# Relative values of an attention block formed in turned layout: two 72-row matmuls of 384 columns instead of six over token tiles

## What is computed

```python
attn_probs = jax.nn.softmax(attn_weights, axis=-1)
attn_output = jnp.einsum('bts,bsd->btd', attn_probs, v)
rel_v = _get_relative_embeddings(emb_rel_v, src_len)
rel_weights = _abs_to_rel(attn_probs)
attn_output = attn_output + jnp.einsum('btm,md->btd', rel_weights, rel_v[0])
out = attn_output.reshape(bsz, H, tgt_len, D).transpose(0, 2, 1, 3).reshape(bsz, tgt_len, E)
return out @ Wo + bo
```

## Time and profile before

| | |
|---|---|
| median of 3 runs | 1387.92 us (1380.27 to 1393.97) |
| profiled execution | 1391.63 us, of which the span 1389.6 us |
| mean granted TensorE clock in it | 0.907 |
| busy: PE / PEld / DVE / ACT / POOL | 83 / 58 / 54 / 27 / 17% |
| chain that ended last | PE 31%, issue 28%, DVE 15%, DMA 12%, SPq 5%, ACT 5% |

### The profile page before, as it was taken

The page is one execution under the profiler, slowest core; times in us unless marked ns, Lnnn a source line. Parts: engine busy times, 40 slices in busy tenths (PEclk is TensorE's granted clock), DMA queues, the critical chain, the costliest instruction groups (busy, mean ns, idle before and its releaser), DMA issues.

```text
span 1389.6 us, 16995 instructions
## 1 busy us (share of the span) xinstructions
PE 1160.2 (83%) x5732; PEld 811.2 (58%) x5732; DVE 751.2 (54%) x1579; ACT 370.3 (27%) x599; POOL 234.4 (17%) x258
## 2 busy tenths in 40 slices
PE   5447699878898898988899788987889888997798
PEld 4212378426784377735785267843777357852588
DVE  6337264763548545573556635475455735466333
ACT  1214212062222522043220622115120432206111
POOL 5404120040200302022200402004020212004000
PEclk9667789988899989999899989999899998999889
DMA  6691207302092102901055020921029010650200
GB/s 210 159 199 62 43 5 128 86 1 59 0 161 52 35 23 57 155 1 35 23 96 116 5 54 0 162 51 35 23 51 160 1 35 23 100 112 1 46 0 12
DMA packets 126985, 89.59 MB, mean 64 GB/s; under 512 B 67991, under 2 KB 116504, under 8 KB 126522
## 3 DMA queue, kind: packets, MB, share of 16 engines
q1 hardware_dynamic: 126552, 88.05, 31.4%
q0 software_dynamic: 384, 1.05, 0.3%
HBM read 60.36 MB, written 28.71 MB: 64 GB/s over the span
## 4 chain that ended last, share of the span: by engine, by line
PE 31%; issue 28%; DVE 15%; DMA 12%; SPq 5%; ACT 5%; POOL 2%; POOLq 0%; DVEq 0%; ACTq 0%
DMA scratch<-d_band_t 9%; PE S L881 7%; PE S L754 4%; PE S L902 4%; DVE S L1189 4%; PE S L746 4%; SPq L538 4%; PE S L809 4%; ACT scratch L999 3%; DVE maxima L1168 3%; PE S L710 3%; PE S L794 2%; DMA txt_row<-in_L_txt_W_E,txt_idx 1%; PE S L627 1%; DMA w_d<-in_L_ffn_Wu 1%
## 5 line engine op out<-in xcount | busy, mean ns | idle before, releaser
L1168 DVE TENSOR_REDUCE maxima<-S 128x2 f32<-128x768 f32 x192 | 176.0, 953 | 82.1 <-PE S L754 80.6
L1432 POOL TENSOR_TENSOR bands<-scratch,one 64x432 f32<-64x432 f32 x128 | 119.5, 934 | 585.8 <-ACT scratch L999 580.7
L902 PE MATMUL S<-w_d,hT 128*128 128x256 f32 x768 | 198.6, 412 | 8.1 <-DVE hT L1306 8.1
L902 PEld LDWEIGHTS S<-w_d,hT 128*128 128x128 f32 x768 | 158.6, 210 | 34.1 <-issue 10.8
L746 PE MATMUL S<-k_st,q_st 128*128 128x384 bf16 x384 | 137.1, 357 | 49.1 <-DMA scratch<-d_band_t 34.7
L1189 DVE TENSOR_TENSOR S<-S,bands 64x144 f32<-64x144 f32 x384 | 154.3, 402 | 43.9 <-PE S L794 34.2
L999 ACT ACTIVATE scratch<-S 128x768 f32<-128x768 f32 x192 | 155.6, 811 | 56.5 <-DVE S L1189 49.1
L1037 ACT ACTIVATE silu<-S 128x384 f32<-128x384 f32 x128 | 62.9, 491 | 396.4 <-PE S L881 309.9
L754 PE MATMUL S<-scratch,ident_b 128*128 128x132 bf16 (+1 forms) x384 | 154.5, 402 | 0.0
L1306 DVE TENSOR_TENSOR hT<-silu,S 128x384 f32<-128x384 f32 x128 | 70.6, 552 | 117.9 <-PE S L881 115.7
L794 PE MATMUL S<-q_st,k_st 128*128 128x384 bf16 x384 | 93.2, 342 | 36.4 <-ACT scratch L999 34.8
(11 more groups left out here) (159 smaller groups left out, 1578.4 us busy)
## 6 DMA issues: line engine op xcount, KB each, us to landing
bands<-d_band_s SPq DMA_DIRECT2D x16, 864.0 KB, 8.8
scratch<-d_band_t SPq DMA_DIRECT2D x8, 1632.0 KB, 16.9
d_parts<-scratch SPq DMA_DIRECT2D x48, 192.0 KB, 2.0
q_st<-d_parts SPq DMA_DIRECT2D x48, 192.0 KB
k_st<-d_parts SPq DMA_DIRECT2D x48, 192.0 KB
d_band_w<-bands SPq DMA_DIRECT2D x32, 240.0 KB, 3.8
out<-scratch SPq DMA_DIRECT2D x8, 384.0 KB, 2.7
x_in<-in_x SPq DMA_DIRECT2D x8, 256.0 KB, 3.7
```

The costliest lines, as they stand in the source:

```text
L902: mm = pe.matmul(D[:, i // 2, (i % 2) * E:(i % 2 + 1) * E], hT[:, (FT * e + m) % 3, i * P:(i + 1) * P], w_d[:, e, m, :], start=(m == 0), s ...
L1168: dve.tensor_reduce(dst, S[:, c0:c0 + 2, PAD:PAD + T], AX, ALU.max).then_inc(max_done.sem, 1)
L1432: nc.gpsimd.tensor_tensor(bands[rows, :, :, 2 * pair:2 * pair + 2].rearrange("p i w h -> p h i w"), win, one[rows].unsqueeze(2).unsqueeze( ...
```

## The change

The relative weights are now scaled into two halves of 8 heads (`rel_p`, 72 = 9 x 8 columns each) with two multiplies, each half is turned with three 72-column transposes (`REL_BANKS`) and copied to `rwt[:, g]` on 72 partitions. One table `rel_v` of 72 rows and 128 columns serves both halves. It is the stationary operand now, and the turned weights are the moving one: one matmul of 384 columns for a half, whose result has channels on partitions and tokens on columns. `attn` is turned before, in a step `turn_attn` that has moved ahead of `turn_weights`, and VectorE adds the relative values onto the turned `attn_t`, with two adds of 384 columns. `FILL_OUT` spreads the same ten units anew. `residual` on TensorE waits for the adds. The list of the round's end is then: `turn_outputs`, gate 13, up 13, gate 14, `turn_attn`, up 14, down 6 part 0 and 1, gate 15, up 15, `turn_weights`, down 7 part 0, `rel_values`, down 7 part 1, `store`. On VectorE `hidden(15)` comes behind `turn_weights` and before `rel_values`, and the accumulate of down 7 part 0 behind `rel_values`.

```diff
-FILL_OUT = [("turn_outputs", 6), ("turn_weights", 2), ("rel_values", 2), ("turn_attn", 0)]
+FILL_OUT = [("turn_outputs", 3), ("turn_attn", 5), ("turn_weights", 1), ("rel_values", 1)]
...
-        rel_v0 = sb("rel_v0", [P, AH, AD])
-        rel_v1 = sb("rel_v1", [RJ - P, AH, AD])
+        rel_v = sb("rel_v", [HJ, HH, AD])
...
-        rel_w = zone(0, TT, RJ)
-        rwt0, rwt1 = zone(512, T), zone(896, T, rows=RJ - P)
+        rel_w, rel_p = zone(0, TT, RJ), zone(1280, TT, KT, HJ)
+        rwt = zone(512, KT, T, rows=HJ)
...
-        REL_TILES = ((0, S[:, 0, 0:E]), (1, S[:, 2, 0:E]), (2, O[:, 0:E]))
+        REL_BANKS = (O, S[:, 2])
...
+            def turn_attn(b):
+                turned(attn, att_dve, 2 * TT, at_pe, b)
+
             def turn_weights(b):
-                pe.wait_ge(att_dve.sem, att_dve.at(b, 2 * TT + 1))
-                for i in range(TT):
-                    last = turn(O[:, i * P:(i + 1) * P], rel_w[:, i, 0:P])
-                last.then_inc(rw_pe.sem, 1)
-                for i in range(TT):
-                    last = turn(S[0:RJ - P, 1, i * P:(i + 1) * P], rel_w[:, i, P:RJ])
-                last.then_inc(rw_pe.sem, 1)
+                for g in range(KT):
+                    pe.wait_ge(att_dve.sem, att_dve.at(b, 2 * TT + g + 1))
+                    for i in range(TT):
+                        last = turn(REL_BANKS[g][0:HJ, i * P:(i + 1) * P], rel_p[:, i, g])
+                    last.then_inc(rw_pe.sem, 1)
 
             def rel_values(b):
-                pe.wait_ge(rw_act.sem, rw_act.at(b, 2))
-                for i, dst in REL_TILES:
-                    pe.matmul(dst, rwt0[:, i * P:(i + 1) * P], rel_v0[:].rearrange("p h d -> p (h d)"),
-                              start=True, stop=False)
-                    pe.matmul(dst, rwt1[:, i * P:(i + 1) * P], rel_v1[:].rearrange("p h d -> p (h d)"),
-                              start=False, stop=True).then_inc(or_pe.sem, 1)
-
-            def turn_attn(b):
-                turned(attn, att_dve, 3 * TT + 1, at_pe, b)
+
+                pe.wait_ge(at_act.sem, at_act.at(b, KT))
+                for g in range(KT):
+                    pe.wait_ge(rw_act.sem, rw_act.at(b, g + 1))
+                    pe.matmul(S[:, g, 0:T], rel_v[:].rearrange("p h d -> p (h d)"), rwt[:, g],
+                              start=True, stop=True).then_inc(or_pe.sem, 1)
 
             def residual(b):
-                pe.wait_ge(at_act.sem, at_act.at(b, 2))
+                pe.wait_ge(att_dve.sem, att_dve.at(b, 2 * TT + 2 * KT))
 
                 pe.wait_ge(acc_done.sem, acc_done.at(b - 1, NE * TT))
...
             def turn_weights(b):
-                act.wait_ge(rw_pe.sem, rw_pe.at(b, 1))
-                nc.scalar.activation(rwt0, O[:, 0:T], ACT.Copy).then_inc(rw_act.sem, 1)
-                act.wait_ge(rw_pe.sem, rw_pe.at(b, 2))
-                nc.scalar.activation(rwt1, S[0:RJ - P, 1, 0:T], ACT.Copy).then_inc(rw_act.sem, 1)
+                for g in range(KT):
+                    act.wait_ge(rw_pe.sem, rw_pe.at(b, g + 1))
+                    nc.scalar.activation(rwt[:, g], REL_BANKS[g][0:HJ, 0:T], ACT.Copy).then_inc(rw_act.sem, 1)
...
-                for dst, rows, n in ((rel_v0, emb_v_rows0, P), (rel_v1, emb_v_rows1, RJ - P)):
-                    dve.tensor_tensor(dst[:], rows[0:n].unsqueeze(1).broadcast_to([n, AH, AD]),
-                                      head_of_rel[0:n].unsqueeze(2).broadcast_to([n, AH, AD]), ALU.mult
-                                      ).then_inc(consts, 1)
+                dve.tensor_tensor(half_head, head_of_rel[0:HJ, 0:HH], head_of_rel[0:HJ, HH:AH], ALU.add
+                                  ).then_inc(half_mask, 1)
+                dve.wait_ge(half_mask, 1)
+                dve.tensor_tensor(rel_v[:], emb_v_rows.unsqueeze(1).broadcast_to([HJ, HH, AD]),
+                                  half_head.unsqueeze(2).broadcast_to([HJ, HH, AD]), ALU.mult
+                                  ).then_inc(consts, 1)
...
                 dve.wait_ge(relw_in.sem, relw_in.at(b, TT))
                 by_j = rel_w.rearrange("p i (j h) -> p i j h", j=NJ)
-                dve.tensor_tensor(by_j, by_j, rden.unsqueeze(2).broadcast_to([P, TT, NJ, AH]), ALU.mult
-                                  ).then_inc(att_dve.sem, 1)
+                for g in range(KT):
+                    heads = slice(g * HH, (g + 1) * HH)
+                    dve.tensor_tensor(rel_p[:, :, g].rearrange("p i (j h) -> p i j h", j=NJ), by_j[:, :, :, heads],
+                                      rden[:, :, heads].unsqueeze(2).broadcast_to([P, TT, NJ, HH]), ALU.mult
+                                      ).then_inc(att_dve.sem, 1)
 
             def rel_values(b):
-                for n, (i, rel) in enumerate(REL_TILES):
-                    dve.wait_ge(or_pe.sem, or_pe.at(b, n + 1))
-                    dve.tensor_tensor(attn[:, i], attn[:, i], rel, ALU.add).then_inc(att_dve.sem, 1)
+                for k in range(KT):
+                    dve.wait_ge(at_act.sem, at_act.at(b, k + 1))
+                    dve.wait_ge(or_pe.sem, or_pe.at(b, k + 1))
+                    dve.tensor_tensor(attn_t[:, k], S[:, k, 0:T], attn_t[:, k], ALU.add).then_inc(att_dve.sem, 1)
```

More of the change, by code:

```diff
@@ L59 @@
 RJ = NJ * AH
+HH = AH // KT
+HJ = NJ * HH
 BPITCH = BL * ROW + BL * AH
@@ L72 @@
 N_ZERO = 8
-N_CONSTS = 8
+N_CONSTS = 7
 FILL_MIX = [("residual", 0), ("mix_in", 0), ("turn_x2", 0), ("mix_sums", 0), ("router", 1),
@@ L213, in fusion_block @@
         emb_k_rows = zone(7640, NJ)
-        emb_v_rows0, emb_v_rows1 = zone(7656, AD), zone(7672, AD)
+        emb_v_rows, half_head = zone(7656, AD, rows=HJ), zone(7672, HH, rows=HJ)
         rel_log_b = Z[:, 4272:4272 + TT * RJ // 2].bitcast(BF16).rearrange("p (i r) -> p i r", i=TT)
@@ L248, in fusion_block @@
         temp_inverse, wr_high, consts = sem("temp_inverse"), sem("wr_high"), sem("consts")
+        half_mask = sem("half_mask")
         gu_high, gu_low, pool_consts = sem("gu_high"), sem("gu_low"), sem("pool_consts")
@@ L281, in fusion_block @@
         ot_pe = sig("ot_pe", TT)
-        or_pe = sig("or_pe", TT)
-        att_dve = sig("att_dve", 3 * TT + 1)
+        or_pe = sig("or_pe", KT)
+        att_dve = sig("att_dve", 2 * TT + 2 * KT)
         at_pe, at_act = sig("at_pe", 2), sig("at_act", 2)
@@ L464, in _ @@
             for j in range(NJ):
-                rows = slice(AH * j, AH * (j + 1)) if j < P // AH else slice(0, AH)
-                at = emb_v_rows0 if j < P // AH else emb_v_rows1
-                groups[2].append((at[rows], dram(emb_v, j * AD, (0, AH), (1, AD))))
+                groups[2].append((emb_v_rows[HH * j:HH * (j + 1)], dram(emb_v, j * AD, (0, HH), (1, AD))))
             def load(g):
```

## The result

The changed kernel takes 1347.84 us (median of four, 1337.55 to 1361.19) against 1390.16 for the kernel before: ratio 0.970, interval 0.965 to 0.975. The forecast was 1351, range 1335 to 1371. The ratios in this document leave out an execution that took over 1.5% more than the fastest of its kernel (here the profiled one, further down one of the run with the accumulate first), the medians do not. The profiled execution took 1361.19 us, the longest of the four, with a span of 1359.4 and a mean granted clock of 0.896 (before: 0.907).

The account below looks back on a forecast made before the run. TensorE led at 83% of the span, with the last accumulate setting the round's end in six rounds; gains of 7.1 + 6 x 4.4 + 5.1 = 38.6 us gave 1351 us, range 1335 to 1371 with the rivals.

Parts of the forecast that it names:

- down 7 starts: Steady round's end: TensorE starts the last down matmuls at +11.87 us, 0.12 behind hidden(15), which now precedes the adds.
- relative matmuls: Steady round's end: two f32 matmuls of 384 columns, four records, take 1.4 us, between bounds of 1.29 and 2.03.
- projection: End of a steady round: the output projection waits for the last accumulate and starts at +17.2 us, before at +22.31.
- L646: Matmuls after the output projection: still released by x_in, 5.04 us behind the last accumulate, at +22.1 us instead of +26.51.
- round 0, gain to the projection: First round, without FFN work and at clock 0.50: output projection at 162.2 instead of 169.30, a gain of 7.1 us.
- sum of the round ends: Whole execution: 7.1 us in round 0, 4.4 in each of six rounds, 5.1 in the last, 38.6 in all.
- first rival: Clock falls in TensorE's new gaps around the output projection, 12 us given back, 1363 us; chance 0.18.
- The rounds get longer elsewhere: One sign that the prediction is wrong: rounds lengthen outside the changed end; no size given.
- the rest is the handover, the shorter matmuls and the turning: Steady round's gain of 4.4 us: about 1.8 is the clock in down 7, these three are the remainder.
- second rival: Round's end: only matmuls get cheaper, down 7 stays at half clock and the adds cost fully; 18.3 us gained, 1371; chance 0.07.
- third: Rival: shifted FFN tiles meet more clock falls; four more a round make it 9 us slower, 1399 us; chance 0.03.
- fourth: Rival: rel_w lands at +11, not +7.6, holding VectorE's multiplies; 0.55 us a round, 1355; forecast including it has chance 0.70.

Follow-up runs that it names:

- run with the accumulate first: Changed kernel with VectorE's accumulate of down 7 part 0 moved ahead of the two adds of the relative values: 1339.9 us, ratio 0.963 to the kernel before.
- run with ScalarE's queue: Changed kernel with x_in and txt_idx issued by ScalarE's queue instead of SP behind the store: 1327.9 us, ratio 0.958 to the kernel before; again 1327.2, 0.959.
- 1358: Trace of the unedited changed kernel measured once more, execution 1357.61 us; that measurement's median was 1357.6 us, ratio 0.981 to the kernel before.
- 1349: Second profile of the unedited changed kernel, execution 1348.66 us; the repeat measured 1351.7 us, ratio 0.976 to the kernel before.
- the old spread: Changed kernel with its FFN units spread as before (6, 0, 2, 2), so hidden(15) is behind the adds: 1345.2 us, ratio 0.970; again 1348.9, 0.974.
- the moved handover: Kernel before with one unit moved, so down 7 part 0 follows turn_weights and hidden(15) precedes the relative adds: 1381.0 us, ratio 0.994.

## Why the prediction was right

Step by step, all times from the first transpose of the outputs:

| step | predicted | measured |
|---|---|---|
| up 14 starts | +5.15 | +5.10 |
| two multiplies of 216 | 0.37 each | 0.375 mean |
| weights' transposes start | +10.99 | +10.94 |
| down 7 starts | +11.87 | +11.88 |
| relative matmuls | 1.4 | 1.29 |
| projection | +17.2 | +17.06 |
| L646 | +22.1 | +21.8 to +22.1 |
| round 0, gain to the projection | 7.1 | 8.5, 6.4, 7.0 |
| sum of the round ends | 38.6 | 41.3 and 39.8 |

- The chain in a steady round was right in its order, in what hides what, and in what is late next: `x_in`, which the run with ScalarE's queue shows.
- The relative values came out at the lower bound: 72 rows after 128 cost nothing. I had added 0.1 for it.
- Round 0 varies with `rel_w`: it lands 7.5 us behind the first transpose in the trace with the gain of 8.5, 9.7 and 9.0 in the other two, and 9.2 in the kernel before. The forecast of 7.1 took it at the old place.
- **The first rival was priced at the wrong place.** I looked for the fall over the projection. There it never came: 1.00 over it in all steady rounds of the three traces. But the falls of the clock lie elsewhere in the unchanged stretches, and that gives back 11 us (execution 1361) or 6 (1358), or gains 3 (1349). "The rounds get longer elsewhere" was one of the signs of being wrong that the prediction named, and two of three traces show it. The gain of the medians was 42, 36 and 27 us in the three measurements, for 38.6 counted. That the ends gave about 40 is the mechanism; that the total came as near as it did is in part luck. The three medians lie around the forecast's 1351, and its range of 1340 to 1362 holds them.
- **A row of the first rival was misread.** It took the 3.87 us of L646 in round 0 for half clock. The half clock was over L852 in front of it; over L646 the clock was 0.94:

```profile
174.58:178.45 3.87, 3.87 (x19) 3.68 (x19) 2.23 (x9) 0.38 (x1) 1.22 (x3) 0.94 0.01 2
```

  What was concluded, that a fall there costs next to nothing, holds by other rows: behind a wait L646 takes 4.10 us at 0.92 (before) and at 0.63 (after).
- **Wrong in the reasoning, though not in the number:** "the rest is the handover, the shorter matmuls and the turning" gave the handover and the clock in down 7 a share each. They are not independent. With the new layout the old spread keeps its wait of 1.26 us and yet has full clock in down 7; with the old layout the moved handover gives the full clock too. Either brings it back, so it cannot be added to both.
- The second rival (only the matmuls get cheaper, 1371) and the third (slower) fell: down 7 is at full clock in all steady rounds of the three traces of the changed kernel. The fourth (`rel_w` late) happened in part and cost nothing: `rel_w` landed between +8.1 and +9.8 in seven of 21 steady rounds, and VectorE's multiplies, which start at +9.4 anyway, waited for it once, 0.28 us.

What stays open: why the falls come at one place in one round and at another in the next, and what brought the clock down over down 7 in the kernel before. It is shown that they come, and what they cost. The old spread with the new layout kept the stretch from maxima to scores at full clock in twelve of fourteen rounds, where the changed kernel did in two of twenty-one; why was not looked into.

## What to carry to other kernels

Count the end of a stage from the instruction that the next stage's DMA waits behind, not from TensorE's last matmul: here the accumulate, and behind it the queue of SP, set the round, and giving the transfer to a queue that was free gained 13 us at the ends of the rounds, a third of what the whole change gained there, and 20 to 30 in total. Look for a contraction whose matmuls have a number of rows that costs no gap next to their neighbours: two matmuls of 72 rows beat 128 and 16 by more than their columns say. And where a short wait is followed by matmuls at half clock, look at the stretch in front of the wait too before blaming the wait.

## What the runs showed of the hardware

- Changing a matmul's rows cost 0.19 us at 2.4 GHz from 64 to 8 and back, from 8 to 128, and between 128 and 16 in the kernel before; from 128 to 64 it cost 0.09, and between 128 and 72 rows nothing (1.29 us for four records of 384 columns, as for other such records).
- The clock fell behind L646 with TensorE busy 3.70 us of 3.70 and no gap before it: a stretch can look full in the busy column and still be followed by half clock. L646's 16 records take 4.10 us behind a wait, at a mean clock of 0.92 or of 0.63, and 3.79 without one at 1.00. The clock hardly enters their time.
- One kernel's median moved between 0.970 and 0.981 of the kernel before on the same chip, with a changed stretch that repeats within 0.3 us from round 1 on. Between its traces the difference lies in stretches over which the clock differs: 31.6 us at 1.00 are 33.4 to 34.5 at 0.90. An edit of 0.45 us a round could not be told from this with `x_in` already moved (1327.0 and 1327.2).
